# Three of twelve context chunks weighed in a decoder layer by fp32r products of halves

## The reference

```python
q = (Q @ WQ).reshape(N, ql, HEADS, DK)
k = (K @ WK).reshape(N, kl, HEADS, DK)
v = (V @ WV).reshape(N, kl, HEADS, DV)
compat = jnp.einsum('nqhk,nlhk->nhql', q, k) / math.sqrt(DK)
weights = jax.nn.softmax(compat, axis=3)
attn = jnp.einsum('nhqk,nkhv->nqhv', weights, v).reshape(N, ql, HEADS * DV)
return attn @ WO + bO
```

## Time and profile before

| | us |
|---|---|
| profiled execution, its own time | 1573.7 |
| its span | 1571.9 |
| median of three runs | 1571.7 |
| TensorE busy | 1515.6 (96%) |
| TensorE weight loads | 1094.0 (70%) |
| VectorE busy | 1123.9 (71%) |
| ScalarE busy | 905.5 (58%) |
| GpSimd busy | 792.8 (50%) |

### The profile page before, as it was taken

One profiled execution on the slowest core, in us unless ns is written; L12 is line 12 of the kernel. 1 busy time (PEld: TensorE's weight loads), 2 busy tenths in 40 slices (PEclk: granted clock), 3 DMA queues, 4 the chain that ended last, 5 costly groups with the idle time before them and its releaser, 6 DMA issues.

```text
span 1571.9 us, 25217 instructions
## 1 busy us (share of the span) xinstructions
PE 1515.6 (96%) x7579; PEld 1094.0 (70%) x7579; DVE 1123.9 (71%) x1816; ACT 905.5 (58%) x1238; POOL 792.8 (50%) x407
## 2 busy tenths in 40 slices
PE   6988999999999999999999999999999999999897
PEld 3446667777777777777777777777777777777485
DVE  4338785868686878778786868686868686987756
ACT  4235675656666666666566666566656666665421
POOL 2002374555556565656555555555555556665611
PEclk9997998999999999999999999999999999999999
DMA  4100010100000000000000000100000000110000
GB/s 154 37 6 15 1 40 38 40 29 38 27 37 30 38 39 39 39 39 39 39 39 39 39 39 39 39 39 35 37 27 38 27 37 33 40 40 20 0 1 24
DMA packets 15251, 54.92 MB, mean 35 GB/s; under 512 B 1111, under 2 KB 6314, under 8 KB 15214
## 3 DMA queue, kind: packets, MB, share of 16 engines
q1 hardware_dynamic: 15214, 54.46, 9.2%
HBM read 53.54 MB, written 0.92 MB: 35 GB/s over the span
## 4 chain that ended last, share of the span: by engine, by line
PE 81%; DVE 9%; ACT 5%; issue 3%; POOL 1%; DMA 0%; DVEq 0%; POOLq 0%; ACTq 0%
PE ps L735 33%; PE ps L701 27%; PE ps L591 3%; PE ps L596 3%; PE ps L582 3%; DVE arena L1300 3%; PE ps L575 3%; PE ps L794 2%; ACT arena L992 2%; PE ps L715 2%; PE ps L511 1%; POOL arena L443 1%; ACT arena L892 1%; PE ps L723 1%; ACT arena L894 1%
## 5 line engine op out<-in xcount | busy, mean ns | idle before, releaser
L1286 DVE TENSOR_TENSOR arena<-arena,ps 125x896 f32<-125x896 f32 x336 | 363.4, 1081 | 98.4 <-PE ps L701 98.1
L443 POOL TENSOR_TENSOR arena<-arena,ring 125x896 f32<-125x896 f32 x192 | 417.6, 2175 | 17.4
L701 PE MATMUL ps<-q_hi,ctxT_hi 128*125 128x448 f32 x768 | 400.5, 522 | 2.5 <-ACT arena L986 1.0
L443 POOL TENSOR_TENSOR arena<-arena 125x896 f32<-125x896 f32 x112 | 236.8, 2114 | 316.2 <-ACT arena L992 307.2
L735 PE MATMUL ps<-ring,ctx_nat 125*128 125x448 f32 x768 | 345.3, 546 | 0.0
L986 ACT ACTIVATE ring<-ps 125x896 f32<-125x896 f32 x192 | 176.5, 919 | 238.9 <-PE ps L735 149.4
L701 PE MATMUL ps<-q_hi,ctxT_lo 128*125 128x448 f32 x768 | 281.7, 367 | 0.0
L701 PE MATMUL ps<-q_lo,ctxT_hi 128*125 128x448 f32 x768 | 281.6, 367 | 0.0
L735 PE MATMUL ps<-arena,ctx_nat 125*128 125x448 f32 x576 | 242.9, 544 | 2.4
L1300 DVE TENSOR_TENSOR ring<-ring,ps 125x896 f32<-125x896 f32 x192 | 201.6, 1078 | 0.0
L701 PEld LDWEIGHTS ps<-q_hi,ctxT_hi 128*125 128x125 f32 x768 | 144.2, 188 | 64.3 <-issue 47.3
(11 more groups left out here) (204 smaller groups left out, 1926.8 us busy)
## 6 DMA issues: line engine op xcount, KB each, us to landing
ctx_raw<-in_ctx_dram SPq DMA_DIRECT2D x32, 750.0 KB
ctx_nat<-in_ctx_dram SPq DMA_DIRECT2D x32, 750.0 KB
w_sb<-in_L_ffn_W_dram SPq DMA_DIRECT2D x1, 1024.0 KB
resid<-in_x_dram SPq DMA_DIRECT2D x1, 896.0 KB, 6.2
out_dram<-ctx_raw SPq DMA_DIRECT2D x4, 224.0 KB, 2.5
ctx_raw<-in_L_xattn_WQ_dram SPq DMA_DIRECT2D x1, 512.0 KB
w_sb<-in_L_xattn_WK_dram SPq DMA_DIRECT2D x1, 512.0 KB
w_sb<-in_L_xattn_WV_dram SPq DMA_DIRECT2D x1, 512.0 KB
```

The lines of the kernel that those rows point to most:

```text
L443: g.tensor_tensor(summed, chunk[0] if j == 1 else summed, chunk[j], ALU.add).then_inc(s["prob_added"], 1)
L701: m = mm(score_ps[j % 2][:, half, :], cx[k][:, rows], q[k][:, cols], start=(n == 0), stop=(n == 2))
L1286: v.tensor_tensor(run_max, kept(k, 0) if j == 1 else run_max, score_ps[j % 2], ALU.max).then_inc(s["maxed"], 1)
```

## The change

Chunks 7, 9 and 11 (`SPLIT`) are weighed in another way, in all periods but the last. ScalarE copies the chunk's probabilities to an fp32r buffer `p_hi`, GpSimd subtracts that from the probabilities to make `p_lo`, right after its own addition of the chunk. At the end of a period GpSimd makes `ctx_hi` and `ctx_lo` for the three chunks of the next sequence's context. TensorE then makes three fp32r products for each half: ctx_hi x p_hi, ctx_lo x p_hi, ctx_hi x p_lo. The first two stand where the fp32 product of their half stood, and the two with `p_lo` come at the end, behind the second half. `p_hi` and `p_lo` are single buffers: the copy for chunk 9 waits until chunk 7 is weighed, that for 11 until 9 is. The four sums of an odd period move from slots 9 and 10 to slots 10 and 11, behind the later additions. To make room, the normalized tokens lose their own buffer: they lie in the last six chunk buffers (now `late_ring`) before the loop, and for the last layer norm in two groups of four tiles in the space of the turned weights; the rows of gamma and beta move too.

The diff, cut to its core ("..." marks what is left out):

```diff
-        xnorm = sb("xnorm", [TOK, PAIRS, D])
+        p_hi, p_lo = [sb(name, [CR, 2, HALF], F32R) for name in ("p_hi", "p_lo")]
+        ctx_hi, ctx_lo = [sb(name, [CR, NS, D], F32R) for name in ("ctx_hi", "ctx_lo")]
...
-        ring += [sb(f"ring{n}", [CR, 2, HALF])[:] for n in range(len(ring), CH)]
+        late_ring = sb("late_ring", [128, (CH - len(ring)) * HQ])
+        ring += [late_ring[0:CR, n * HQ:(n + 1) * HQ].rearrange("p (a b) -> p a b", a=2) for n in range(CH - len(ring))]
+        xnorm_first = late_ring[0:TOK, 0:PAIRS * D].rearrange("p (k d) -> p k d", k=PAIRS)
...
         PLACES = (".... .... .... .... .... .... t.p. t.p. t.p. ..p. .... ....",
-                  ".... .... .... .... .... .... t... t.q. t.q. q.qs sss. ....")
...
-        LAST_PLACES = {(PAIRS - 2, 1): ".... .... .... .... .... .... t.x. t.x. t.l. l.xs lsss ....",
+                  ".... .... .... .... .... .... t... t.q. t.q. q.q. .sss s...")
...
+        LAST_PLACES = {(PAIRS - 2, 1): ".... .... .... .... .... .... t.x. t.x. t.l. l.x. lsss s...",
...
+        LOW_AFTER = {7: 7, 9: 9, 11: 11}
...
+        def split_chunks(i, k):
+            return () if isinstance(i, int) and i == PAIRS - 1 and k == 1 else SPLIT
...
+        def halves_free(b, j):
+            n = SPLIT.index(j)
+            return CH * b + (SPLIT[n - 1] + 1 if n else 0)
...
+            def context_halves(i, k):
+                nb = 2 * i + k
+                chunks = slice(SPLIT[0], SPLIT[-1] + 1, SPLIT[1] - SPLIT[0])
+                need(pool, f"nat_in{k}", 16 * (i + 1))
+                need(pool, "weighted", CH * nb)
+                g.tensor_tensor(ctx_hi[:], ctx_nat[k][:, chunks, :], ones[0:CR, None, :].to_broadcast((CR, NS, D)), ALU.mult).then_inc(s["ctx_hi_done"], 1)
+                need(pool, "ctx_hi_done", nb + 1)
+                g.tensor_tensor(ctx_lo[:], ctx_nat[k][:, chunks, :], ctx_hi[:].bitcast(F32), ALU.subtract).then_inc(s["ctx_lo_done"], 1)
+            def low_probability(b, k, j):
+                need(pool, "prob_hi_done", split_count(b, j))
+                g.tensor_tensor(p_lo[:], kept(k, j), p_hi[:].bitcast(F32), ALU.subtract).then_inc(s["prob_lo_done"], 1)
...
                     g.tensor_tensor(summed, chunk[0] if j == 1 else summed, chunk[j], ALU.add).then_inc(s["prob_added"], 1)
+                    if j in LOW_AFTER and LOW_AFTER[j] in split_chunks(i, k):
+                        low_probability(b, k, LOW_AFTER[j])
...
+                if not (isinstance(i, int) and i == PAIRS - 1):
+                    context_halves(i + k, 1 - k)
...
-                    m = tr(ps[:, banks[q], t * TOK:(t + 1) * TOK], xnorm[:, G4 * q + t, :], ident[0:TOK, 0:TOK])
+                    m = tr(ps[:, banks[q], t * TOK:(t + 1) * TOK], normed(count, G4 * q + t), ident[0:TOK, 0:TOK])
...
-                if half == 0 or j == 0:
-                    need(pe, "prob_done", step_count(b, j, half))
-                m = mm(usum_ps[:, half, :], ctx_nat[k][:, j, :], kept(k, j)[:, half, :], start=(j == 0), stop=(j == CH - 1))
+                if j in split_chunks(i, k):
+                    n = SPLIT.index(j)
+                    if half == 0:
+                        if n == 0:
+                            need(pe, "ctx_lo_done", b + 1)
+                        need(pe, "prob_hi_done", split_count(b, j))
+                    for cx in (ctx_hi, ctx_lo):
+                        mm(usum_ps[:, half, :], cx[:, n, :], p_hi[:, half, :], start=False, stop=False)
+                    if half == 1:
+                        need(pe, "prob_lo_done", split_count(b, j))
+                        for part in range(2):
+                            m = mm(usum_ps[:, part, :], ctx_hi[:, n, :], p_lo[:, part, :], start=False, stop=(j == CH - 1))
+                else:
+                    if half == 0 or j == 0:
+                        need(pe, "prob_done", step_count(b, j, half))
+                    m = mm(usum_ps[:, half, :], ctx_nat[k][:, j, :], kept(k, j)[:, half, :], start=(j == 0), stop=(j == CH - 1))
...
+            def high_probability(b, k, j):
+                need(act, "prob_done", step_count(b, j))
+                need(act, "weighted", halves_free(b, j))
+                a(p_hi[:], kept(k, j), ACT.Copy).then_inc(s["prob_hi_done"], 1)
...
+                    if j > SPLIT[0] and j + 1 in split_chunks(i, k):
+                        high_probability(b, k, j + 1)
...
                     if j and not last:
                         keep_scores(b + 1, 1 - k, j)
+                    if j == SPLIT[0] - 2 and split_chunks(i, k):
+                        high_probability(b, k, SPLIT[0])
                     for n in EXPS_AT.get(j, ()):
                         exponential(b, k, n)
...
+                if count == 3:
+                    need(dve, "xT_ps", 2 * GROUPS + q - 1 if q > 1 else 0)
```

More of the change, by code:

```diff
@@ L177, in decoder_layer @@
         yT_sb = [cut(GT) for n in range(2)]
+        rows_b = cut(2 * D, TOK).rearrange("p (n d) -> p n d", n=2)
         seen = sb("seen", [TOK, PAIRS])
@@ L668, in self_attention @@
                 for t in range(G4):
[L669 removed]
+                    m = mm(ps[0:TOK, SELF_BANK[q], t * D:(t + 1) * D], gauss_wT[:, G4 * q + t, :], normed(1, G4 * q + t), start=True, stop=True)
                 m.then_inc(s["self_attn_ps"], 1)
@@ L1081, in period @@
                         a(b1_r[0:E, 0, :], b1_sb[:], ACT.Copy).then_inc(s["b1_hi_done"], 1)
-                assert not slot_work(i, k, CH - 1) or last
+                assert last or all(what == "sums" for what, _, _ in slot_work(i, k, CH - 1))
             sequence(act, period)
```

19 lines of the change are left out of this document (13 added, 6 removed).

## The result

The changed kernel takes 1589.17 us (median of 4 runs, 1588.41 to 1593.56), the one before 1571.6 us: a ratio of 1.0106, 95% interval 1.0089 to 1.0122. It is slower, by 1.1%; the forecast was 1553.5. The profiled execution has a span of 1586.6 us, 14.7 more than the 1571.9 of before.

A forecast was written before the change was run, and what follows sets the result against it. TensorE's stream was taken to bound the loop: 27.0 us of cheaper products, less 3.9, 3.7 and 1.2 of waits, gave 18.2 us saved, 1555.5 profiled or 1553.5 us median. Range 1545 to 1570, likeliest 1549 to 1559.

The forecast's parts named there:

- Part 1: TensorE's products: six fp32r products for each split chunk save 0.29 us, 27.0 us gross over 93 chunks.
- Rival E: TensorE's new products run closer together than all others: 36 us gross, 27 net, 1545 us; chance 0.03.
- Rival D: TensorE's products don't get cheaper, since fp32r and fp32 alternate in one accumulation: 1572 to 1576 us; chance 0.06.
- Part 2: ScalarE's three more copies a period, 2.8 us, stay hidden; chunk 7's in odd periods by 1 us.
- Part 3: GpSimd's three subtractions a period, 2.18 or 3.01 us each, hidden except chunk 7's in odd periods: 3.9 us lost.
- rival A: GpSimd's new subtractions are slow, 3.01 us each: 18 us slower, 1590 us; chance 0.15 with whatever else is slower.
- Part 4, the even seam: End of even periods: shorter weighing no longer hides VectorE's run maximum; 0.06 of 0.29 us stay, 3.7 us lost.
- odd seam: End of odd periods: 2.67 us of TensorE's sums and weighings hide 2.3 us of VectorE's work before the turn.
- Part 4, the end: Near the end TensorE's two waits, 1.1 us after period 28 and 1.9 in period 30, swallow 1.2 us of gains.

The follow-up runs named there:

- e8: Kernel before plus only ScalarE's three copies a period in periods 28 to 30, read by nobody, nothing split: 1579.7 us, ratio 1.0023.
- e5: Changed kernel splitting chunks 7 and 9 in even periods, 7, 9 and 11 in odd ones, up to period 27: 1579.4 us, ratio 1.0015 to before.
- e4: Changed kernel with GpSimd subtracting only 8 of 448 columns after period 0: 1586.1 us, ratio 1.0088 to the kernel before.
- e1: Changed kernel with chunks split in periods 0 to 27 only, the last three weighed in fp32: 1569.7 us, ratio 1.0005 to the kernel before.
- e2: Changed kernel with chunks split in periods 28 to 30 only: 1592.0 us, ratio 1.0134 to the kernel before.
- e9: Changed kernel, nothing split, no ScalarE copies; only GpSimd's subtractions and context halves in periods 28 to 30, unread: 1593.0 us, ratio 1.0103 to before.
- e6: As e5, but split from period 2 to 27 only: 1568.5 us, ratio 0.9952 to the kernel before.
- e10: e6 with the odd periods' sums back in their old slots: 1563.5 us, ratio 0.9929 to the kernel before.
- e14: e10 with the sums of period 1 alone in the last two slots: 1553.0 us, ratio 0.986 to the kernel before.

## Why the prediction was wrong, step by step

- **Part 1, right.** Products 0.20 us apart, 0.29 us a chunk: an odd period without a wait is 42.07 against 42.95. Rival E asked for 0.19, and no product of the new kind shows it. Rival D is out. The Trainium skill's spacing (TensorE: Matmul & The Clock Gate, "Back-to-back issue gap") gives 0.19 us too, and the trace disagrees here as it did before.
- **Part 2, right in the loop, wrong at the end.** No wait in the loop falls on a copy. In period 28 the copy of chunk 7 goes ahead of the transposed context, and VectorE starts 0.84 us late (e8).
- **Part 3, the step that failed.** A subtraction costs 2122 ns, what I took, so rival A's price is wrong; that its total of 1590 came out is luck. I had read the earlier trace rows in one direction: GpSimd's add took 3.01 us beside VectorE's queries, so GpSimd is slowed. I never asked what a subtraction that starts first does to VectorE. It costs 0.76 us in each even period (39.11 to 39.87), about 10 us in the loop. In period 28 GpSimd holds VectorE up by 4.8 of the 5.7 us, 1.8 of them behind subtractions, the rest behind an addition, a power and the context halves. In odd periods the same reading erred to the other side. I had charged 0.26 for chunk 7, and VectorE waited in TensorE's place, at no cost: 0.88 gained, not 0.61.
- **Part 4, the even seam, right and covered up.** I said that chunk 11 would keep only 0.06 of its 0.29 in an even period. It kept nothing: e5, without it, and e4, with it, both take 39.11. The edit there bought nothing, and its subtraction brought the loss. That the odd seam is hidden was right for the change, by virtue of the moved sums.
- **Part 4, the end, the largest miss.** I wrote off 1.2 us for the two waits of the earlier trace rows. A wait of 1.1 us for VectorE says that VectorE sets the pace there; what is put in its way then counts nearly whole (5.7 us of VectorE, 5.4 us of period 28). The waits of the three periods grew by 11.7 us, and 11.9 more went as the granted clock fell behind the long ones. That all of it hangs on the split in these periods is shown (e1, e2), and that GpSimd's work suffices for most of it too (e9).
- **The clock.** No case of mine had it. It takes back gains in loops with no wait at all (e4, e5, e6), and in the traces it goes with the place of the sums (e6 against e10, e10 against e14). Why the last slots bring falls in the loop and take one away in period 1 is open. That e14 comes out at 1553.0 us, the very forecast, is chance: it splits less, and 6.0 of its 20.5 us are clock in period 1.

## What to carry to other kernels

Before work goes to an idle GpSimd, list VectorE's instructions beside it that read two SBUF operands or scale from SBUF to SBUF, and price each at up to one GpSimd instruction late, whatever its own size; a stretch in which TensorE already waits for VectorE takes no such work. With the last three periods left out the edit went from 1% slower to no change (e1); with chunk 11 of the even periods and the first two periods left out too, to 0.5% faster (e6); with the sums in their old slots but in period 1, to 1.4% (e14). When a part is shown to gain and the total does not, read the granted clock slice by slice before looking for another wait.
